# Cross-attention block in float32: attention outputs normalised before the projection, and every second score unit's maxima added by VectorE

## What is computed

```python
def _attention(xq, xkv, wq, wk, wv, wo, bo):
    q, k, v = (xq @ wq), (xkv @ wk), (xkv @ wv)          # split into 16 heads of 64
    attn = jnp.einsum('bihd,bjhd->bhij', q, k) * scale
    attn = jax.nn.softmax(attn, axis=-1)
    out = jnp.einsum('bhij,bjhd->bihd', attn, v).reshape(B, S, D_ATTN)
    return out @ wo + bo
h = _layernorm(x, ln1_g, ln1_b)
x = _attention(h, h, sa_wq, sa_wk, sa_wv, sa_wo, sa_bo) + x
h = _layernorm(x, ln2_g, ln2_b)
x = _attention(h, cond_emb, ca_wq, ca_wk, ca_wv, ca_wo, ca_bo) + x
h = _layernorm(x, ln3_g, ln3_b)
p = h @ ff_w1 + ff_b1
return (p[..., :D_FF] * gelu(p[..., D_FF:])) @ ff_w2 + ff_b2 + x
```

## Time and profile before

| | us |
|---|---|
| median of 3 runs (1217.2 to 1218.09) | 1217.85 |
| the profiled execution | 1216.59 |
| its span in the trace | 1214.5 |
| TensorE busy | 1186.0 |
| VectorE busy | 764.5 |
| GpSimd busy | 742.7 |
| ScalarE busy | 642.1 |

### The profile page before, as it was taken

The page is one execution under the profiler, slowest core; times in us unless marked ns, Lnnn a source line. Parts: engine busy times, 40 slices in busy tenths (PEclk is TensorE's granted clock), DMA queues, the critical chain, the costliest instruction groups (busy, mean ns, idle before and its releaser), DMA issues.

```text
span 1214.5 us, 23620 instructions
## 1 busy us (share of the span) xinstructions
PE 1186.0 (98%) x9385; PEld 777.0 (64%) x9385; DVE 764.5 (63%) x1289; ACT 642.1 (53%) x954; POOL 742.7 (61%) x381
## 2 busy tenths in 40 slices
PE   4999999999999999999999999999999999999998
PEld 3655666666666566666666655666666666678887
DVE  5767567567566576575675666368777877764433
ACT  4457544444454446744444544467765586536432
POOL 2397797786786876877977868864555436321000
PEclk9999999999999999999999999999999999999999
DMA  3000000000000000000000000011211110100000
GB/s 112 15 27 10 15 15 10 15 15 10 6 15 19 5 11 23 6 10 23 6 10 13 20 4 5 23 32 50 58 38 25 33 33 18 20 27 18 18 18 18
DMA packets 63539, 25.76 MB, mean 21 GB/s; under 512 B 34551, under 2 KB 61383, under 8 KB 63431
## 3 DMA queue, kind: packets, MB, share of 16 engines
q1 hardware_dynamic: 63375, 24.25, 7.7%
q10 hardware_dynamic: 56, 0.01, 0.0%
HBM read 21.62 MB, written 2.10 MB: 20 GB/s over the span
## 4 chain that ended last, share of the span: by engine, by line
PE 89%; POOL 4%; ACT 3%; DVE 2%; issue 1%; DMA 0%; SPq 0%; DVEq 0%; POOLq 0%; ACTq 0%
PE psum L829 22%; PE psum L815 22%; PE psum L707 15%; PE psum L692 9%; PE psum L852 7%; PE psum L792 6%; POOL acc L1373 4%; PE psum L912 4%; PE psum L840 3%; PE psum L797 2%; PE psum L866 1%; ACT probs L1244 1%; DVE xr L1055 1%; DVE m_part L1018 1%; ACT h_hi L1164 0%
## 5 line engine op out<-in xcount | busy, mean ns | idle before, releaser
L1373 POOL TENSOR_TENSOR acc<-acc,probs 128x1024 f32<-128x1024 f32 x192 | 458.7, 2389 | 70.1 <-ACT probs L1244 49.7
L1244 ACT ACTIVATE probs<-psum 128x1024 f32<-128x1024 f32 (+1 forms) x320 | 317.1, 1031 | 275.6 <-PE psum L815 272.7
L1018 DVE TENSOR_REDUCE m_part<-psum 128x2 f32<-128x1024 f32 x256 | 308.9, 1222 | 222.9 <-PE psum L792 222.9
L829 PE MATMUL psum<-probs,val 128*64 128x512 f32 x1024 | 244.9, 604 | 0.0
L1373 POOL TENSOR_TENSOR acc<-probs 128x1024 f32<-128x1024 f32 (+1 forms) x64 | 152.8, 2388 | 142.2 <-ACT probs L1244 120.2
L1055 DVE SCALAR_TENSOR_TENSOR xr<-psum,d_cols,xr 128x256 f32<-128x256 f32 x512 | 207.8, 476 | 35.0 <-PE psum L852 34.5
L829 PEld LDWEIGHTS psum<-probs,val 128*64 128x64 f32 x1024 | 63.3, 136 | 113.7 <-issue 98.8
L815 PE MATMUL psum<-row_max,minus 64*128 64x512 f32 (+1 forms) x640 | 126.0, 389 | 0.0
L815 PE MATMUL psum<-q_hi,k_hi 64*128 64x512 f32 x512 | 101.7, 393 | 0.3 <-DVE m_part L1018 0.3
L815 PE MATMUL psum<-q_hi,k_lo 64*128 64x512 f32 x512 | 101.0, 389 | 0.0
L815 PE MATMUL psum<-q_lo,k_hi 64*128 64x512 f32 x512 | 100.9, 389 | 0.0
(11 more groups left out here) (147 smaller groups left out, 2130.3 us busy)
## 6 DMA issues: line engine op xcount, KB each, us to landing
xr<-in_x SPq DMA_DIRECT2D x8, 256.0 KB, 5.4
wqk_raw<-in_L_xattn_sa_wq SPq DMA_DIRECT2D x16, 128.0 KB, 2.5
wqk_raw<-in_L_xattn_sa_wk SPq DMA_DIRECT2D x16, 128.0 KB, 2.4
wv_raw<-in_L_xattn_sa_wv SPq DMA_DIRECT2D x8, 256.0 KB, 3.0
wo_raw<-in_L_xattn_sa_wo SPq DMA_DIRECT2D x16, 128.0 KB, 2.4
d_cols<-d_rows SPq DMA_DIRECT2D x128, 2.0 KB, 2.1
wqk_raw<-in_L_xattn_ca_wq SPq DMA_DIRECT2D x16, 128.0 KB, 2.5
probs<-in_L_xattn_ff_w SPq DMA_DIRECT2D x8, 256.0 KB, 3.5
```

Source lines behind the costliest of these rows:

```text
L829: mm = pe.matmul(psum[d, PVB + half, :], values(J)[0:plan.ks, kt, own], probs[buffer_of(J, u)][0:plan.ks, h, :], start=(kt == 0), stop=(kt ...
L1018: dve.tensor_reduce(m_part[:, half, :, t, kh], psum[:, bank0:bank0 + 2, :], AX.X, ALU.max).then_inc(s_x_read, 1)
L1244: act.activation(probs[buffer_of(J, u)][0:plan.ks, :, :], psum[0:plan.ks, bank0:bank0 + 2, :], ACT.Exp, scale=SCALE).then_inc(s_exp, 1)
L1373: pool.tensor_tensor(total, last if kt == 1 else total, now, ALU.add).then_inc(s_acc, 1)
```

## The change

Two things change, and the written order of all engines with them.

1. The maxima. They are reduced negated. In the self stage M now stores them to DRAM, and a new step N reads them back spread over all 128 partitions (less_max, 512 KB per half iteration). In units 1, 3, ... 15 of a self iteration the fourth pair of matmuls is gone; a new VectorE step U adds less_max to the scores and writes them to the buffer of the exponentials, and ScalarE takes the exponential there in place. Even units, and all cross units, keep a fourth pair with a row of +1.
2. The denominators. E now copies the whole output, unnormalised (o_raw). B's reciprocals are stored to DRAM and read back spread over 64 partitions per head (spread_d), R multiplies, Z (ScalarE) takes the hi part, L the lo part, both from SBUF. The projection then accumulates both heads in one bank, in two turns as Q does, and VectorE adds two blocks of 128x1024 to xr instead of 16 scaled ones.

```diff
+TAKEN_BY_VECTOR = (1, 3, 5, 7, 9, 11, 13, 15)
+def on_vector(J, u):
+    return J < NSELF and u in TAKEN_BY_VECTOR
...
 SELF_ORDER = {
-    "sp": "G++@-58.84 O@9.97 T-@10.13 W++@12.95 M1@38.05 M0+@40.90",
+    "sp": "O0@47.029 G0@49.587 W0@50.429 M0@104.465 N0@122.559 M1@141.291 N1@166.499 T0@175.090 B0@200.314 R0@219.910",
...
             def move_m(J, a):
...
+                if own:
+                    sp.dma_start(max_rows[a].rearrange("h (p t) -> p h t", p=P),
+                                 m_cols[a][:].bitcast(F32).rearrange("p (h t) -> p h t", h=2)).then_inc(s_m[a], 16)
+                    return
...
+            def spread_m(J, a):
+                sp.wait_ge(s_m[a], MOVED[J + 1])
+                if J:
+                    sp.wait_ge(s_s, U0[J - 1] + 8 * (a + 1))
+                    sp.wait_ge(s_taken, taken(J - 1, 8 * (a + 1)))
+                sp.dma_start(less_max[a][:].bitcast(F32), max_rows[a].partition_broadcast(P)).then_inc(s_less_max[a], 16)
...
+            def store_recip(J):
+                sp.wait_ge(s_recip, J + 1)
+                after(sp, s_d_spread, 32 * J)
+                sp.dma_start(d_recip_rows.rearrange("h a (p t) -> p (h a) t", p=P),
+                             d_cols[J % 2][:].rearrange("p (r t) -> p r t", r=4)).then_inc(s_d_recip, 16)
+
+            def spread_recip(J):
+                sp.wait_ge(s_d_recip, 16 * (J + 1))
+                after(sp, s_o_full, J)
+                for h in range(2):
+                    sp.dma_start(spread_d[h * DH:(h + 1) * DH, :, :], d_recip_rows[h].partition_broadcast(DH)).then_inc(s_d_spread, 16)
...
+                last = 2 if on_vector(J, u) else 3
+                for i, (w, x) in enumerate(((k_hi, q_hi), (k_hi, q_lo), (k_lo, q_hi))):
                     for h in range(2):
...
+                if last == 3:
+                    for h in range(2):
+                        x = less_max[half][rows_of(h), h, :] if plan is SELF else top[J % 2][rows_of(h), qs]
+                        mm = pe.matmul(psum[0:plan.ks, bank_of(("S", J, u), h), :], one_row[rows_of(h), 0:plan.ks], x, start=False, stop=True)
...
+            def take(J, u):
...
+                dve.wait_ge(s_s, U0[J] + u + 1)
+                dve.tensor_tensor(probs[buffer_of(J, u)][:], psum[:, bank0:bank0 + 2, :], less_max[half][:].bitcast(F32), ALU.add).then_inc(s_taken, 1)
+
+            def R(J):
+                dve.wait_ge(s_d_spread, 32 * (J + 1))
+                dve.wait_ge(s_o_raw, 2 * J + 2)
+                o = o_full(J).rearrange("k h (t p) -> k h t p", t=4)
+                dve.tensor_tensor(o, o, spread_d[:].rearrange("k h (p t) -> k h t p", t=4), ALU.mult).then_inc(s_o_full, 1)
+
+            def L(J):
+                dve.wait_ge(s_o_hi, J + 1)
+                dve.tensor_tensor(o_low(J)[:], o_full(J), o_hi[:], ALU.subtract).then_inc(s_o_lo, 1)
...
-                        op = dve.scalar_tensor_tensor(x, psum[:, bank, t * DM:(t + 1) * DM], d_cols[J % 2][:, c0:c0 + 1], x, ALU.mult, ALU.add)
...
+                dve.tensor_tensor(x, x, psum[:, bank0:bank0 + 2, :].rearrange("p k (t d) -> p (k t) d", t=2), ALU.add).then_inc(s_y_done, 1)
...
+                if on_vector(J, u):
+                    act.wait_ge(s_taken, taken(J, u) + 1)
+                    act.activation(p, p, ACT.Exp, scale=SCALE).then_inc(s_exp, 1)
+                    return
...
+            def Z(J):
+                act.wait_ge(s_o_full, J + 1)
                 if J:
...
+                    wait_prep(act, ("Y", J - 1, 1))
...
+                act.activation(o_hi[:], o_full(J), ACT.Copy).then_inc(s_o_hi, 1)
```

244 lines of the change are left out of this document (141 added, 103 removed), and 38 rows, old and new, of tables (CROSS_ORDER, OPENING, SELF_ORDER, TURN).

## The result

The changed kernel takes **1356.72 us** (median of 4 runs, 1354.46 to 1358.79) where the kernel before takes 1217.55 on the same chip: ratio 1.1142, 95% interval 1.1128 to 1.1155. It is 11% slower; 1206 was predicted, and the range ended at 1224. The profiled execution has a span of 1354.6 us.

What follows compares the result with a forecast made beforehand. TensorE's issued work was taken as the bound: 1216.59 - 29.4 + 2.8 + 3.0 + 6.0 + 2.0 + 4.1 = 1205.1 us, and with the runs' median 1.26 above the profiled execution, 1206 us; range 1189 to 1224.

Steps and rivals of the forecast that it cites:

- The taken maxima, -29.4: Self iterations: dropping 128 fourth matmul pairs at 0.23 us each saves 29.4 us of TensorE work, the whole gain.
- The new shapes: VectorE's new 128x1024 steps, self iterations: priced by the nearest reduce at about 1.2 us each, 36 us busy of about 45.5.
- The walk from D to R: Self iteration: spread lands 11.2 to 11.9 us after D, R ends at 14.2; TensorE stalls 0.4 us, 6.0 in all.
- the slower rival: Self iterations: the spread lands later, R misses the gap between GpSimd adds and ends 2.4 us later; 1242 us, chance 0.16.
- the prediction's own sign of failure: Self iteration: the forecast falls if the spread lands over 13 us after D.
- The price of that rival: Self iterations, slower rival: 15 x 2.4 = 36 us as U7, X2, L and Y follow R, 1242 us.
- The exclusion: VectorE instructions with both operands in SBUF (R, L) wait until a running GpSimd add ends; R waits from 12.3 to 13.1.
- The cross stage, 0, bounds 0 to 7: Cross iterations: VectorE is relieved and L ends 0.8 us before TensorE reaches Y, so 0 us added.
- Opening +2.0: Opening: later first weights 0.6 us and a later first unit 1.4 us, together 2.0, bounds 0 and 4.
- end +4.1: End of the cross stage: stalls of 2.4 us for Y30 and 1.7 for Y29, 4.1 us, bounds 1 and 8.
- VectorE as second bound: Rival, self iterations: VectorE's queue runs 0.5 to 0.8 us later than counted, 10 us more, 1216; no-change chance 0.09.
- The maxima's own detour: Spread of the first maxima takes 6.0 instead of 2.0 us, hidden behind about 9 us of TensorE work, 3 to spare.

Runs made afterwards that it cites:

- run 3: Changed kernel without the multiply R and with reciprocals stored and spread only for iteration 0, outputs not normalised: 1225.41 us, ratio 1.0068.
- run 4: Changed kernel with no units taken by VectorE, all maxima added by TensorE's fourth matmul pair again: 1386.81 us, ratio 1.1396.
- 9: Kernel before with only the maxima part, eight taken units per self iteration in a second placing (0, 1, 3, 8, 10, 12, 13, 14): 1223.54 us, ratio 1.0051.
- 13: Kernel before with only the maxima part, eight units in the second placing, iteration 0 left to TensorE: 1227.09 us, ratio 1.0095.
- 14: Kernel before with only the maxima part, eight units from iteration 1 on, iteration 0's maxima moved straight into one SBUF row: 1224.72 us, ratio 1.0059.
- run 5: Kernel before with only the maxima part, eight taken units per self iteration in a first placing (1, 3, 7, 9, 11, 12, 13, 15): 1281.21 us, ratio 1.0520.
- run 1: Changed kernel with R reading and writing whole rows instead of a stride of four elements, outputs wrong: 1323.05 us, ratio 1.0862.
- run 2: Changed kernel with reciprocals stored to DRAM and spread only for iteration 0, later multiplies reusing those values: 1270.78 us, ratio 1.0427.
- run 8: Changed kernel with GpSimd's adds cut to 64 of 512 columns from iteration 1 on, denominators wrong: 1330.24 us, ratio 1.0931.
- run 11: Kernel before with VectorE holding one PSUM pair 2.44 us longer in 14 self iterations: 1260.55 us, ratio 1.0352.

## Why the prediction was wrong, point by point

- **The taken maxima, -29.4.** Right here as TensorE's work: without R an iteration takes 45.8 us, as forecast (run 3), and taking the units back costs 30.1 us (run 4; that this agrees so closely is in part luck, as said there). Not a gain by itself: in the kernel before, taking eight units per iteration brings 0.4 us in the median iteration and nothing in all (runs 9, 13, 14). The term counted TensorE's work and left out that each taken unit reaches its exponential 1.2 us later (run 5).
- **The new shapes.** U, Z and Y as priced. **R failed**: 1.22 us came from an instruction that reads whole rows. Alone it takes 1.98 (the shortest of 32 executions), 1.22 with whole rows (run 1). The order of elements in its second operand stood in the diff. (The Trainium skill, SBUF — State Buffer, section Door 1: The DMA port swizzle, says that an access that goes on to a new line of 16 bytes pays a penalty; a stride of four fp32 elements does so each time, and the trace agrees: 1.98 against 1.22 us. The same note gives four fp32 elements as a stride that is still free; there the measurement decides against it.)
- **The walk from D to R.** The reciprocal began 4.68 us after D, as counted (4.7). The store was counted 2.0 and took 3.0 to land; the spreads were issued 3.16 us after it. The two were counted 4.2 together (0.6 and 3.5) and ended 5.7 after their issue. **This failed**: the spread landed 13.9 us after D (13.7 to 15.4 in the self iterations), not 11.2 to 11.9. Two steps with no row, each priced at the nearest one, added over 2 us. The gap between two GpSimd additions was counted at 13.1 and lay at 13.5; R missed it and ended at 17.8, not 14.2. That is the slower rival, step by step, and the prediction's own sign of failure (a spread over 13 us after D). It had the rival at a chance of 0.16.
- **The price of that rival.** 2.4 us per iteration and 1242 in all. R's end moved by 2.44 us between run 2 and the changed kernel, and the self iteration by 2.85: right in size. But R that meets the gap isn't free either, as the forecast had it (0.4 us of stall): the self stage of run 2 is 32.8 us longer than that of run 3, 2.2 per iteration. Together the self stage lost 75.6 us in 15 iterations, 5.0 each: TensorE idles 2.9 us more, and its matmuls take 2.2 us longer. **The clock was missing from the whole sum.** In a kernel that keeps TensorE at 1.00 a gap isn't worth its length alone (run 11: 1.8 costs 3.1).
- **The exclusion.** Right as a mechanism: R ends a fixed 1.8 us behind a GpSimd addition in every self iteration but the last, as the subtract of the earlier trace rows did with 0.54. Wrong in size where it matters: R was counted to lose 0.7 us to it; in the self stage R is 1.4 us longer on average than with short additions (run 8). The mean over all 32 multiplies, 0.73, agrees with the 0.7 by luck, as in most cross iterations no addition holds R up.
- **The cross stage, 0, bounds 0 to 7.** It lost 64.1 us, the largest error (by D; Y30's few microseconds have moved out of this stage). By the runs: the detour 39.4 (after less run 2), R 11.5 (2 less 3), and 13.2 that the rest of the normalisation costs there with no multiply at all. I had counted VectorE's load, which falls, and the arrival at Y, but not what stands behind R in VectorE's order: the Q subtracts, which free the banks for the next maxima, and on ScalarE the next row copy behind Z, by which one late spread makes the next one late.
- **Opening +2.0 and end +4.1.** The opening measured +4.9, above its bound of 4. The end term stood for TensorE's waits ahead of Y29 and Y30, 1.7 and 2.4 us. They are in the trace with 2.25 and 3.65 us, 5.9 together, inside the bounds of 1 and 8. The +11.0 of the last stage is not that term: it holds Y30's matmuls as well, and 6.4 of it is there without R too (run 3).
- **VectorE as second bound.** In the self stage it is busy 573 of 770 us, 74%, near the 36 of 45.5 that were counted. It isn't full, but it is in order: TensorE's 26.5 us of waits for U come about as in the rows above, where U stands behind R.
- **The maxima's own detour** was hidden in the iterations of the changed kernel, as forecast: TensorE's long waits name U and not its spread.

With store and spread sized right, the count would have given the slower case, 1242, and with R's stride 12 us more in the self stage (15 x 0.8), 1254. The other 100 us or so are what it left out: the cross stage above all, the clock behind each wait, and the rest of what R costs where it meets the gap.
